# Local attention with 192 probability columns per head: three transposed banks and an edge block fetched by DMA

## The reference, cut to what matters

```
bk, bv = (look_around(bk), look_around(bv))      # keys of [window before, own window]
sim = jnp.einsum('bhwid,bhwjd->bhwij', bq, bk)
mask = (i < j) | (i > j + WINDOW) | (j == -1)
sim = jnp.where(mask, -jnp.finfo(sim.dtype).max, sim)
attn = jax.nn.softmax(sim, axis=-1)
out = jnp.einsum('bhwij,bhwjd->bhwid', attn, bv)
```

## Time and profile before

| | us |
|---|---|
| median of three runs | 1901.61 |
| profiled execution | 1904.1 |
| its span on the core | 1902.3 |
| PE busy | 1846.5 (97%) |
| DVE busy | 1478.6 (78%) |
| ACT busy | 1103.0 (58%) |
| POOL busy | 431.6 (23%) |
| DMA, mean of the span | 24 GB/s |

### The profile page before, as it was taken

The page is one execution under the profiler, slowest core; times in us unless marked ns, Lnnn a source line. Parts: engine busy times, 40 slices in busy tenths (PEclk is TensorE's granted clock), DMA queues, the critical chain, the costliest instruction groups (busy, mean ns, idle before and its releaser), DMA issues. The chain is left out here.

```text
span 1902.3 us, 48194 instructions
## 1 busy us (share of the span) xinstructions
PE 1846.5 (97%) x17316; PEld 1605.9 (84%) x17316; DVE 1478.6 (78%) x4483; ACT 1103.0 (58%) x2551; POOL 431.6 (23%) x318
## 2 busy tenths in 40 slices
PE   8999999999999899999999999999999999989998
PEld 7879888889888788888888788877888888878887
DVE  5877867777767688888888777768888888877777
ACT  4543433433433488888988434438888888853333
POOL 0000000000000355545543000014445444501111
PEclk9999999999999999999999999999999999999999
DMA  9200000000010100000000200010000000000002
GB/s 323 72 1 2 1 1 2 1 2 1 1 70 1 52 7 4 6 6 6 4 6 11 88 12 12 11 45 5 6 6 4 6 6 6 4 23 12 12 11 94
DMA packets 47060, 44.74 MB, mean 24 GB/s; under 512 B 12479, under 2 KB 41451, under 8 KB 46958
## 3 DMA queue, kind: packets, MB, share of 16 engines
q1 hardware_dynamic: 46958, 43.33, 7.0%
HBM read 34.93 MB, written 8.39 MB: 23 GB/s over the span
## 5 line engine op out<-in xcount | busy, mean ns | idle before, releaser
L1125 ACT ACTIVATE l_probs<-l_probs,l_negmax 128x256 f32<-128x256 f32 x512 | 253.4, 498 | 83.5 <-DVE l_negmax L1235 83.5
L1083 POOL TENSOR_TENSOR l_t<-l_t,l_rnorm 128x512 f32<-128x512 f32 x128 | 131.1, 1046 | 295.2 <-DVE l_rnorm L1252 295.2
L1078 POOL TENSOR_TENSOR l_t<-l_t,l_t 128x1024 f32<-128x1024 f32 x64 | 153.2, 2394 | 126.6 <-DVE l_t L1287 126.6
L117 PE MATMUL ps<-local_w_hi,l_xT 128*128 128x512 f32 x384 | 165.2, 430 | 6.7 <-DVE l_xT L1195 3.4
L118 PE MATMUL ps<-local_w_lo,l_xT 128*128 128x512 f32 x384 | 151.9, 396 | 0.0
L119 PE MATMUL ps<-local_w_hi,l_xT 128*128 128x512 f32 x384 | 151.1, 394 | 0.0
L1413 PE MATMUL ps<-ident,l_probs 128*128 128x128 f32 x1024 | 145.5, 279 | 1.7 <-ACT l_probs L1125 1.4
L499 ACT ACTIVATE attn_exp<-ps 128x512 f32<-128x512 f32 x128 | 76.5, 600 | 116.8 <-PE ps L119 116.8
L117 PE MATMUL ps<-m_hnT_hi,ffn_w_hi 128*128 128x512 f32 (+1 forms) x352 | 141.0, 401 | 0.0
L118 PE MATMUL ps<-m_hnT_lo,ffn_w_hi 128*128 128x512 f32 (+1 forms) x352 | 138.4, 393 | 0.0
L119 PE MATMUL ps<-m_hnT_hi,ffn_w_lo 128*128 128x512 f32 (+1 forms) x352 | 138.3, 393 | 0.0
(11 more groups left out here) (252 smaller groups left out, 5790.0 us busy)
## 6 DMA issues: line engine op xcount, KB each, us to landing
tok_x<-x SPq DMA_DIRECT2D x16, 512.0 KB, 7.9
m_shifted<-shifted SPq DMA_DIRECT2D x20, 256.0 KB, 2.8
shifted<-x SPq DMA_DIRECT2D x64, 64.0 KB, 1.5
out<-x SPq DMA_DIRECT2D x8, 512.0 KB, 4.5
ffn_w_raw<-ffn_w SPq DMA_DIRECT2D x6, 640.0 KB
local_w_raw<-ffn_wqkv SPq DMA_DIRECT2D x4, 768.0 KB, 5.1
tok_base<-attn_base SPq DMA_DIRECT2D x4, 512.0 KB, 9.2
h<-txt SPq DMA_DIRECT2D x4, 512.0 KB, 8.0
```

The lines of the kernel that those rows point to most:

```text
L117: nc.tensor.matmul(out, wh, mh, start=start, stop=False, skip_group_check=True)
L1078: nc.gpsimd.tensor_tensor(t1[:], t1[:], t2[:], ALU.add).then_inc(s.summed.sem, 1)
L1083: nc.gpsimd.tensor_tensor(v, v, rn[:, a * LH:(a + 1) * LH].unsqueeze(2).to_broadcast([P, LH, DH]), ALU.mult).then_inc(s.rotated.sem, 1)
L1125: last = nc.scalar.activation(v, v, ACT.Exp, bias=nb[:, h:h + 1], scale=-1.0, accum_out=rsum[:, h:h + 1])
```

## The change

The 192 live columns alone are masked, exponentiated, transposed and multiplied.

- The probabilities of a pair of heads are now 384 columns in three blocks of 128: the even head's full window (128), the two heads' edge halves (64 + 64), the odd head's full window (128). Which window is the full one depends on the query's half, row by row. `score` writes its products into this layout, as 32 products in both parities; the mask is one table of 320 columns, of which even heads use columns 0 to 191 and odd ones 128 to 319. In steps with r = 1, `mask_even` is now built from it by one instruction over 320 columns instead of one over 128.
- Four pairs make twelve blocks, which are transposed into three banks (`THIRDS`) by twelve transposes in place of sixteen, and leave by three copies of 512 columns on ACT in place of four. TQ+1 is no longer used for them.
- `values` works by halves of the tile: per pair, half and head one product with the full window's values and one with the edge block, 64 columns each. Since the edge block holds both heads, its weights are `edge`, a new tile whose upper 64 rows hold the even heads' values and whose lower 64 rows those of the odd heads, with zeros (a POOL memset at the phase's start) in the other places. 32 products of 64 columns replace 16 of 128.
- SP fills `edge` with four DMAs of 64 KB per tile, SBUF to SBUF: two when the values of the tile are copied (`own_edge`, behind `v_done`), two when `values` has run (`next_edge`, behind `o_full`). `values` waits for them (`edged`).
- To keep the even heads' and the odd heads' values together for those DMAs, the copy of bank V (L1158) reads and writes with permuted patterns of 64 columns.
- The masks come in two loads of 160 KB in place of four of 64 KB.

The order of projection, output product and the rest in the step is as it was. The diff, cut:

```diff
     QK, V, TQ, OT = 0, 2, 3, 7
     XT, RB = 5, 6
-    PT = (XT, RB, TQ, TQ + 1)
+    PT = (XT, RB, TQ)
+    THIRDS = len(PT)
...
+            def edge_of(which, w, tokens):
+
+                for e, rows in enumerate((LOW, HIGH)):
+                    cols = slice(e * LINNER // 2, (e + 1) * LINNER // 2)
+                    sp.dma_start(edge[rows, which, cols], vv[tokens, w, cols]).then_inc(s.edged.sem, 16)
+
+            def own_edge(t, w):
+
+                sp.wait_ge(*s.v_done.after(t + 1))
+                edge_of(0, w, LOW)
+
+            def next_edge(t, w):
+
+                sp.wait_ge(*s.o_full.after(t + 1))
+                edge_of(1, w, HIGH)
...
             with sp.Fori(0, T // 2 - 2) as p:
                 for r in range(2):
+                    own_edge(2 * p + 1 + r, 1 - r)
                     store(p, r)
+                    next_edge(2 * p + 1 + r, 1 - r)
...
             nc.gpsimd.memset(vv[:, 1], 0.0).then_inc(s.set.sem, 1)
+            nc.gpsimd.memset(edge[:], 0.0).then_inc(s.set.sem, 1)
...
-                    v = pm[:, pair, e * 2 * P:(e + 1) * 2 * P]
+                    v = pm[:, pair, e * REACH:(e + 1) * REACH]
                     last = nc.scalar.activation(v, v, ACT.Exp, bias=nb[:, h:h + 1], scale=-1.0,
                                                 accum_out=rsum[:, h:h + 1])
...
-            def probs_out(t, pair):
-                wait(act, s.p_t, 4 * t + pair + 1)
-                nc.scalar.activation(pt[:, pair], ps[:, PT[pair]], ACT.Copy).then_inc(s.p_done.sem, 1)
+            def probs_out(t, k):
+                wait(act, s.p_t, THIRDS * t + k + 1)
+                nc.scalar.activation(pt[:, 4 * k:4 * k + 4].rearrange("p b q -> p (b q)"), ps[:, PT[k]],
+                                     ACT.Copy).then_inc(s.p_done.sem, 1)
...
-                    nc.scalar.activation(vv[:, r], ps[:, V], ACT.Copy).then_inc(s.v_done.sem, 1)
+                    nc.scalar.activation(vv[:, r].rearrange("p (e m d) -> p m e d", e=2, d=DH),
+                                         ps[:, V].rearrange("p (m e d) -> p m e d", e=2, d=DH),
+                                         ACT.Copy).then_inc(s.v_done.sem, 1)
...
-                    chain(nc.vector.tensor_scalar(mask_e[:, P:2 * P], prev[:], negs[:, bass.ds((n - 1) // 2, 1)], None,
-                                                  ALU.add))
+                    chain(nc.vector.scalar_tensor_tensor(mask_e[:], before_sel[:], negs[:, bass.ds((n - 1) // 2, 1)],
+                                                         mask_o[:], ALU.mult, ALU.add))
...
-            def values():
+            def values(own):
 
                 for pair in range(LPAIRS):
-                    for w in range(2):
-                        for e in range(2):
-                            h = 2 * pair + e
-                            last = nc.tensor.matmul(ps[e * DH:(e + 1) * DH, OT, pair * P:(pair + 1) * P],
-                                                    vv[:, w, h * DH:(h + 1) * DH],
-                                                    pt[:, pair, (2 * e + w) * P:(2 * e + w + 1) * P],
-                                                    start=(w == 0), stop=(w == 1))
+                    for half, w in enumerate((1 - own, own)):
+                        tokens = slice(half * DH, (half + 1) * DH)
+                        for kind in range(2):
+                            for e in range(2):
+                                at = e * LINNER // 2 + pair * DH
+                                keys, block = ((vv[:, w, at:at + DH], 2 * e), (edge[:, half, at:at + DH], 1))[kind]
+                                last = nc.tensor.matmul(ps[e * DH:(e + 1) * DH, OT, pair * P + tokens.start:pair * P + tokens.stop],
+                                                        keys, pt[:, 3 * pair + block, tokens],
+                                                        start=(kind == 0), stop=(kind == 1))
                 last.then_inc(s.o_full.sem, 1)
...
                 if c:
-                    for pair in (2, 3):
-                        if b:
-                            wait(pe, s.qk_done, 2 * n - 3 + pair)
-                        else:
-                            wait(pe, s.masked, 4 * (n - 1))
-                        probs_t(n - 2, pair)
+                    if b:
+                        wait(pe, s.qk_done, 2 * n - 1)
+                    else:
+                        wait(pe, s.masked, 4 * (n - 1))
+                    probs_t(n - 2, 2)
...
                     wait(pe, s.v_done, n - 1)
+                    wait(pe, s.edged, 64 * (n - 2) + 32)
                     wait(pe, s.y_done, n - 2)
-                    values()
+                    values(r)
```

More of the change, by code:

```diff
@@ L1157, in step @@
                     wait(act, s.o_full, n - 2)
-                    nc.scalar.activation(vv[:, r], ps[:, V], ACT.Copy).then_inc(s.v_done.sem, 1)
+                    nc.scalar.activation(vv[:, r].rearrange("p (e m d) -> p m e d", e=2, d=DH),
+                                         ps[:, V].rearrange("p (m e d) -> p m e d", e=2, d=DH),
+                                         ACT.Copy).then_inc(s.v_done.sem, 1)
                 if c:
-                    for pair in range(LPAIRS):
-                        probs_out(n - 2, pair)
+                    for k in range(THIRDS):
+                        probs_out(n - 2, k)
                 if piece is not None:
@@ L1235, in score @@
                 last = nc.vector.tensor_tensor_reduce(
-                    pm[:, pair, e * 2 * P:(e + 1) * 2 * P], ps[:, bank, at:at + 2 * P],
-                    mask[:], -8.0, -LOWEST, ALU.add, ALU.min, nb[:, h:h + 1])
+                    pm[:, pair, e * REACH:(e + 1) * REACH], ps[:, bank, at:at + REACH],
+                    mask[:, e * P:e * P + REACH], -8.0, -LOWEST, ALU.add, ALU.min, nb[:, h:h + 1])
                 if e:
@@ L1389, in score @@
                 bank = QK if half == 0 else TQ
-                reach = (((slice(0, 3 * DH),), (slice(DH, 4 * DH),)) if own else
-                         ((slice(2 * DH, 4 * DH), slice(0, DH)), (slice(0, 2 * DH), slice(3 * DH, 4 * DH))))
+                parts = (((1 - own, slice(0, P)), (own, slice(0, P))), ((own, LOW), (1 - own, HIGH)))
+                places = ((0, DH), (P, 0))
                 for pair in (2 * half, 2 * half + 1):
[L1393 to L1396, removed]
+                    for part, place in zip(parts, places):
+                        for qs, (w, keys) in zip((LOW, HIGH), part):
                             for e in range(2):
+                                at = pair % 2 * 2 * P + place[e]
                                 rows = slice(e * DH, (e + 1) * DH)
-                                last = nc.tensor.matmul(ps[qs, bank + e, at + keys.start:at + keys.stop], qt[rows, pair, qs],
-                                                        kt[rows, pair].rearrange("p w t -> p (w t)")[:, keys],
+                                last = nc.tensor.matmul(ps[qs, bank + e, at:at + keys.stop - keys.start],
+                                                        qt[rows, pair, qs], kt[rows, pair, w, keys],
                                                         start=True, stop=True)
@@ L1500, in step @@
                     wait(pe, s.spread, n - 1)
-                    wait(pe, s.p_done, 4 * (n - 1))
+                    wait(pe, s.p_done, THIRDS * (n - 1))
                     inverses()
@@ L1924, in __init__ @@
         self.scored = count("scored")
+        self.edged = count("edged")
         self.masked = count("masked")
@@ L1982, in __init__ @@
         self.ident = aps["ident"]
-        self.mask_cur = aps["mask_cur"]
-        self.mask_prev = aps["mask_prev"]
+        self.mask = aps["mask"]
+        self.mask_sel = aps["mask_sel"]
         self.negs = aps["negs"]
@@ L2143, in build @@
         K.signs = [(K.flags[:], A.flags), (K.negs[:], A.negs)]
-        K.masks = [(K.mask_prev[:], A.mask_prev), (K.mask_o[:, P:2 * P], A.mask_cur), (K.mask_e[:, 0:P], A.mask_cur),
-                   (K.mask_o[:, 0:P], A.mask_prev)]
+        K.masks = [(K.mask_o[:], A.mask), (K.mask_sel[:], A.mask_sel)]
         def tables(layer):
@@ L2210, in arrays @@
     i, j = np.arange(P)[:, None], np.arange(P)[None, :]
-    out["mask_prev"] = np.where(i > j, MASKED, 0.0).astype(np.float32)
-    out["mask_cur"] = np.where(i < j, MASKED, 0.0).astype(np.float32)
+    prev, cur = (np.where(hidden, MASKED, 0.0).astype(np.float32) for hidden in (i > j, i < j))
+    low, high = slice(0, DH), slice(DH, P)
+    out["mask"] = np.concatenate([np.concatenate([prev[low], cur[low, low], prev[low]], 1),
+                                  np.concatenate([cur[high], prev[high, high], cur[high]], 1)])
+    edge = np.arange(2 * P + DH)[None, :] // DH == P // DH
+    out["mask_sel"] = ((i < DH) != edge).astype(np.float32)
     first = np.arange(T // 2) % (TB // 2) == 0
```

37 lines of the change are left out of this document (25 added, 12 removed).

## The result

The changed kernel takes 1905.6 us (median of 7 runs, 1904.4 to 1907.7) against 1901.0 for the kernel before, measured beside it (7 runs, 1897.7 to 1902.8). The ratio is 1.0025, with a 95% interval of 1.0014 to 1.0036: 4.7 us slower. The forecast said 1903.7 and a rise of 2.1. The profiled execution took 1906.1 us, its span 1904.3.

A forecast was written before the change was run, and what follows sets the result against it. PE was taken to wait for ACT's 2.54 us from square to V's copy, transposes giving 0. Values, scores, ends and mask loads: 6.4 + 1.3 - 4.6 - 1.0 = +2.1 us; 1901.6 + 2.1 = 1903.7 us, range 1896 to 1911.

The forecast's parts named there:

- Bound: At the values' projection, PE waits for ACT's copy of V, so four fewer transposes per tile were booked at 0.
- Waits and lengths: Signs in loop steps: load 0.05 us behind V's copy, square to load 2.54, scores 1.50, copy at most 0.62.
- Values: 32 products of 64 columns on PE: +0.10 us per tile, +6.4 us, bounds 0 and 0.13 per tile.
- Ends: Filling and draining each layer: narrower masks and exponentials shorten waits, 2.3 us per layer, -4.6 us, bounds 0 and twice that.
- The step at fault: Filling and draining: 0.07 us saved per narrower mask or exponential, summed over the waits to 2.3 us per layer.
- Mask loads: Start of layer 0, where DVE waits for masks: two loads instead of four, -1.0 us, between 0 and -2.5.
- POOL's memset: Phase starts: the longer memset lies beside the mask wait in layer 0 and is small in layer 1; 0.
- Edge DMAs: Four per tile; two must land within 5.2 us between V's copy and the values: 0 us, 2 us to spare.
- within 0.2%: Whole kernel: time within 3.8 us of the kernel before, given 60%, against 15% faster and 25% slower.
- the rivals: Transposes' gain, 1876, 6%; ends twice, 1897.6, 7%; slower V copy, 1909, 8%; late edge DMAs, 1954, 5%; load-limited values, 2004, 2%.
- the ring: Loop step: queries and keys' projection on PE, ACT's 2.54 us, then PE from values' projection to the next projection.

The follow-up runs named there:

- e1: Kernel before with its fourth group of transposes left out (12 instead of 16): 1903.0 us, ratio 1.0012.
- e7: Changed kernel with its third group of four transposes issued twice (16 again): 1905.9 us, 1.0028 of the kernel before.
- e2: Changed kernel with ACT's copy of V moved in front of the square: 1877.5 us, 0.9880 of the kernel before.
- e6: Changed kernel with V's copy in front of the square and the third group of transposes issued twice: 1901.7 us, 1.0003 of the kernel before.
- e8: Changed kernel with its two mask loads split in four: 1906.1 us, 1.0028 of the kernel before.
- e5: Changed kernel without its four edge DMAs per tile and the values' wait for them: 1904.9 us, 1.0023 of the kernel before.
- e3: Kernel before, 16 transposes kept, with V's copy in front of the square: 1917.4 us, ratio 1.0091.
- e9: Kernel before with 12 transposes and V's copy in front of the square: 1912.6 us, ratio 1.0056.
- e11: Kernel before with values' products of pairs 2 and 3 split in halves (24 products, short ones last): one run, 1908.9 us.
- e10: Kernel before with values' products of pairs 0 and 1 split in halves (24 products, full-width ones last): one run, 1904.3 us.

## Why the prediction was right, point by point

- **Bound.** The largest decision was to book 0 instead of -27 us for the transposes. It rested on 0.05 us between V's copy and a load, seen in rows 1000 us apart. e1, e7, e2 and e6 show it right: the cover is V's copy, and nothing else.
- **Waits and lengths.** Load 0.05 us behind the copy, square to load 2.54 in all loop steps, scores 1.50 in both parities, V's permuted copy 0.62, no wait of the values for a DMA: as written. The idle time in front of the load was put at 0.4 and is 0.49.
- **Values.** +0.10 a tile from 64 small loads elsewhere in the program; measured +0.11 with r = 0 and +0.16 with r = 1. The term of +6.4 was some 2 us short. More than half of that is the bubble at the jump, for which that row, inside straight code, had no sign. The loop's 54 steps cost +9.7 us where the forecast's terms gave 54 x 0.12 = +6.5. Values and scores account for 54 x 0.11 + 27 x 0.05 + 27 x 0.04 = 8.4. The other 1.3 lies in two stretches: from the load of the values' projection to the scores every step takes 0.01 us more (0.6 in all), and from the next projection's load to its square every second step takes 0.02 more (0.6). Neither has a known cause.
- **Ends.** Filling and draining were put at -4.6 us, 2.3 a layer. Layer 1 shows -0.47 - 0.34 - 0.99 = -1.8. In layer 0 the mask loads lie in squares 1 to 3 as well; e1, with four loads and the same granted clock as e8 (0.69), takes 24.85 us there against e8's 24.15 (its missing transposes gain nothing there: 21.58 us in layer 1, 21.59 before), so the ends give -0.70 there and with the other two stretches -2.0; with layer 1's -0.47 in its place it is -1.8. Both layers together give -3.6 to -3.8, some 0.9 less than booked. The step at fault booked each narrower instruction's saving in full at every wait of the ends, and took 0.07 us for an exponential that gave 0.055.
- **Mask loads.** -1.0 was booked. In the profiled pair PE's wait in squares 1 to 3 of layer 0 fell from 3.44 to 1.35 us, so they gave -2.1, and the stretch agrees: -2.54, less the -0.47 that layer 1 shows without such loads. e8 puts them at -2.9 with the clock that PE lost in that execution, beyond the bound of -2.5, which took DVE's wait alone. That this error and the last nearly cancel is luck: -5.6 was forecast for both, -5.6 came.
- **POOL's memset** of `edge`, booked at nothing, goes with the +0.59 at the starts, 0.21 in layer 0 and 0.38 in layer 1. It takes 0.96 us, and a DVE instruction beside it (`l_xT`, 0.22 us in the kernel before) now takes 0.43 in layer 0 and 0.60 in layer 1. Both times it ends 0.02 us behind the memset, and PE's first load waits for it. No run leaves the memset out. In layer 0:

```profile
623.56 0.96 POOL L1092 MEMSET l_edge<- 128x1024 f32 x1
...
624.11 0.43 DVE L1229 TENSOR_SCALAR l_xT<-l_xT,l_flags 128x2 fp32r<-128x2 f32 x1
```

- **Edge DMAs** land in 2.0 us (median), against the 1.5 of the earlier trace rows and far below the 5.2 of room; e5 shows them free.

So the time lies inside the range, on the slow side of the forecast. The likeliest case was "within 0.2%"; measured is +0.25%, with an interval that holds 0.2%, so whether that case came true is undecided. That the kernel became slower is not: the whole interval lies above 1. The rise is twice the forecast's, from the loop (+9.7 against +7.7 for values and scores in all tiles) and the starts (+0.6 against 0).

None of the rivals came true. What they lacked is a case that the experiments add: with V's copy moved as well, the changed kernel is 28 us faster, 0.45 a tile.

## What to carry to other kernels

Before counting what a shorter engine saves, find the release in front of its next step; where the distance from the releaser to the waiting instruction is constant, shortening the waiting engine is worth nothing until the releaser is moved. When such a change comes out neutral, look for where its slack went (here 0.74 us on ACT and 0.49 on PE) and for work in the ring that could have been done a step earlier: the two together gave 23 us, where alone the one lost 5 and the other 16. A slip measured in one kernel (e3's 0.36 us) is no constant; in e9, with PE's product early, it was 0.76, since another ring had closed.

## What the runs showed of the hardware

- PE's busy share is no measure of its slack. It is 96% in the changed kernel, which waits 30.6 us for one copy, and 97% in e2, which doesn't. (The Trainium skill, page "Perfetto Trace Analysis", section "Identifying the Most-Contended Engine", says that matmul occupancy is not a good measure of how close TensorE is to its roofline; here it doesn't tell the slack either.)
- Short products directly in front of a loop's jump cost 0.02 to 0.05 us a pass in one layer and up to 0.35 in the other (1.95 against 2.30 in e11); the same products earlier in the pass cost none of it (e10: 1.96 in all). Why the layers differ is open.
- A 64-column product with its own load costs little: 32 of them 0.11 us more than 16 of 128 columns, 0.007 us for each added pair.
- Two loads of 160 KB were 2.0 us sooner complete than the same bytes in four.
- Which clock PE is granted behind nearly the same wait differed between profiled executions: over 11 us of the first steps of layer 0 it was 0.84 in the kernel before (wait 3.44) and 0.69 in e1 (wait 3.28).
